# Layer 1's four spreads: from four products and copies to one product and four row broadcasts by DMA

## The chip, the core and the metric

The kernel runs on one core of one Trainium2 chip. The metric is device time in microseconds (us) of one execution. TensorE multiplies matrices (PE in the profile, its weight loads PEld), VectorE is DVE, ScalarE is ACT, GpSimd is POOL, and SyncE is SP, which here only issues DMAs.

## The reference, cut to what matters

Sixteen graphs of 512 nodes with 128 features pass through four graph layers, each behind a layer norm and a ReLU and added back to x. Layer 1 is the one that the change is about. Its attention has four heads of 32 features:

```python
h = (node_feats @ W.T + b).reshape(Bb, Nn, Hh, Cc)
l_src = jnp.einsum('bihc,hc->bih', h, a_src)
l_dst = jnp.einsum('bjhc,hc->bjh', h, a_dst)
logits = jax.nn.leaky_relu(l_src[:, :, None, :] + l_dst[:, None, :, :], ALPHA)
logits = jnp.where(adj_matrix[..., None] == 1, logits, NEG_INF)
probs = jax.nn.softmax(logits, axis=2)
out = jnp.einsum('bijh,bjhc->bihc', probs, h)
```

Layer 0 is the same with one head. Layer 2 mixes by sigmoids of products of node rows, layer 3 is three steps of a GRU over summed neighbours. `l_dst` of a head is one row of 512 numbers. The kernel wants that row in all 128 partitions, since partitions are the nodes i; this is the head's "spread".

## The kernel before, in words

One graph is handled in tiles of 128 partitions: four chunks c of 128 nodes, each a row of 512 neighbours. A graph goes through four stages: A (layer 0, bank `a_bank`), L (layer 1, banks `l0_bank` and `l1_bank`), B (layer 2) and C (layer 3). Each engine runs one list of (graph, step), sorted by a number from the tables `BEGIN` and `WHEN`. So the stages of neighbouring graphs interleave: while L of graph g runs, so do A of g+1, B and C of g-1. Nothing but semaphores ties one engine's place in its list to another's, and every engine takes its list strictly in order.

A unit is one head and one chunk, 16 in all for layer 1. For unit n, DVE does step `n` (`masked_max`, L611: spread minus mask, with the row maximum), then, once a head's four maxima are in, the shifts (L617 to L622) and step `v` (`logits`, L625). ACT exponentiates (L435), PE turns the result in an l bank (L879, step `q`), ACT copies it to `pT` (L443). Step `sum` (L968) uses all of it, and `x2` adds it to x.

Layer 1 begins with `stats1`, `norm1`, `rows1` (PE turns the normed rows into `l0_bank`, ACT copies them to `hT1`), then for each head h a step `dst`: PE multiplies `hT1` by `dst_rep[:, h, :]`, whose 128 columns are all the same, so all 128 partitions of the bank get the row (L934), and ACT copies it to one of two `spread` buffers (L427). `values1` (L686 to L693 on DVE) makes the values and the source terms. Heads 3 and 4 wait for a free buffer and a free bank in the middle of the units.

SP issues the loads of x, adj and the turned adj for all graphs, in program order: x of g+2, adj of g+1, turned adj of g. There is one buffer for adj (`adj_i`); `mask0`, `mask1`, `count` and `edges` read it.

## Time and profile before

| what | value |
|---|---|
| three runs | 1105.32, 1108.17, 1108.45 us, median 1108.17 |
| the profiled execution | 1104.81 us, its span 1103.0 us |
| PE busy | 959.7 us (87%) |
| DVE busy | 944.8 us (86%) |
| ACT busy | 885.0 us (80%) |
| POOL busy | 96.1 us (9%) |

The span is what the trace covers; the time holds 1.8 us more around it. The busy shares are means over the fill of the pipeline, thirteen even graphs in the middle, and the drain.

### The profile page before, as it was taken

The page shows a single profiled execution, that of the slowest core. Times are in us where ns is not written, and L with a number is a line of the kernel's source. Part 1 is how long each engine was busy: PE and PEld are TensorE (multiplying, and loading weights), DVE is VectorE, ACT ScalarE, POOL GpSimd, SP SyncE. Part 2 cuts the span into 40 slices and gives each one's busy share as a digit, 9 for nine tenths or more (in the row PEclk, how much of TensorE's full clock was granted, in tenths as well). Part 3 has the DMA queues.
Part 4 walks back from the last instruction along what each step waited for, and adds up shares of the span by engine and source line. Part 5 has one row for each costly group of instructions (what it writes and reads, how often), then busy time and mean ns, then how long its engine had stood idle before and what let it go on. Part 6 is the DMA issues. An engine that isn't in the chain of part 4 may idle for free.

```text
span 1103.0 us, 16049 instructions
## 1 busy us (share of the span) xinstructions
PE 959.7 (87%) x5024; PEld 613.6 (56%) x5024; DVE 944.8 (86%) x2710; ACT 885.0 (80%) x1876; POOL 96.1 (9%) x138
## 2 busy tenths in 40 slices
PE   4677898989989898998989898998989799898875
PEld 3453655656565565656566565656556465655443
DVE  5396989899898989999898989989898998988543
ACT  3477897979889797979889797988979798887643
POOL 0101010010001010100101011010101100000000
PEclk8678999999999999999999999999999999999989
DMA  2101111020111102011111102011110201101000
GB/s 89 50 37 48 39 48 48 11 86 11 39 49 48 49 11 87 10 41 47 48 49 48 50 10 79 18 40 49 48 49 10 87 1 40 48 1 48 1 10 10
DMA packets 34028, 43.92 MB, mean 40 GB/s; under 512 B 1040, under 2 KB 17424, under 8 KB 33936
## 3 DMA queue, kind: packets, MB, share of 16 engines
q1 hardware_dynamic: 25488, 38.61, 11.1%
q10 hardware_dynamic: 8448, 4.20, 1.3%
q8 instruction: 44, 0.72, 0.3%
q14 instruction: 48, 0.39, 0.1%
HBM read 38.61 MB, written 4.19 MB: 39 GB/s over the span
## 4 chain that ended last, share of the span: by engine, by line
PE 47%; DVE 36%; ACT 7%; issue 6%; POOL 3%; DMA 0%; DVEq 0%; ACTq 0%; SPq 0%; POOLq 0%
DVE probs L611 9%; PE l_bank L879 6%; DVE probs L625 6%; PE x_bank L968 5%; PE a_bank L911 4%; DVE sess L781 3%; PE r_bank L1029 3%; DVE sess L774 3%; PE n_bank L1029 2%; PE n_bank L1044 2%; ACT hn L367 2%; PE n_bank L1047 2%; PE l_bank L934 2%; PE r_bank L1032 2%; PE h_bank L1032 2%
## 5 line engine op out<-in xcount | busy, mean ns | idle before, releaser
L625 DVE SCALAR_TENSOR_TENSOR probs<-spread,s_lift,probs 128x512 f32<-128x512 f32 x320 | 232.9, 746 | 1.8
L611 DVE CUSTOM_DVE_ANT_0 probs<-spread,mask 128x512 f32<-128x512 f32 x320 | 211.9, 684 | 3.4 <-ACT spread L427 3.1
L443 ACT ACTIVATE pT<-l_bank 128x512 f32<-128x512 f32 x256 | 153.7, 600 | 40.9 <-PE l_bank L879 40.9
L435 ACT ACTIVATE probs<-probs,shift_p 128x512 f32<-128x512 f32 x256 | 185.0, 723 | 1.0 <-DVE probs L625 1.0
L879 PEld LDWEIGHTS l_bank<-ident,probs 128*128 128x128 f32 x1024 | 123.8, 144 | 78.8 <-issue 40.5
L879 PE MATMUL l_bank<-ident,probs 128*128 128x128 f32 x1024 | 155.0, 277 | 10.0 <-ACT probs L435 9.1
L349 POOL TENSOR_TENSOR rstd<-var_eps,power 128x4 f32<-128x4 f32 x64 | 72.8, 1137 | 961.0 <-DVE var_eps L605 636.3
L367 ACT ACTIVATE hn<-x,shift,rstd 128x128 f32<-128x128 f32 x192 | 79.4, 498 | 34.6 <-POOL shift L351 34.6
L934 PE MATMUL l_bank<-hT,dst_rep 128*128 128x512 f32 x128 | 72.1, 646 | 12.9 <-ACT pT L443 11.0
L427 ACT ACTIVATE spread<-l_bank 128x512 f32<-128x512 f32 x64 | 38.4, 600 | 42.2 <-PE l_bank L934 42.2
L1015 PE MATMUL y_bank<-hn,sess 128*128 128x128 f32 x512 | 64.3, 279 | 8.3 <-DVE sess L781 8.3
L1015 PEld LDWEIGHTS y_bank<-hn,sess 128*128 128x128 f32 x512 | 59.7, 192 | 15.1 <-DVE sess L781 15.1
L911 PE MATMUL a_bank<-values,pT 128*128 128x128 f32 x512 | 62.9, 283 | 0.7 <-ACT pT L400 0.7
L911 PEld LDWEIGHTS a_bank<-values,pT 128*128 128x128 f32 x512 | 61.3, 200 | 1.2 <-ACT pT L400 1.1
L968 PE MATMUL x_bank<-pT,values 128*32 128x512 f32 x512 | 61.2, 620 | 0.7 <-ACT pT L443 0.7
L804 DVE SCALAR_TENSOR_TENSOR hid_n<-r_t,hid_n 128x512 f32<-128x512 f32 x48 | 33.0, 687 | 28.0 <-ACT r_t L493 27.6
L435 ACT ACTIVATION_READ_ACCUMULATOR probs<-probs,shift_p 128x1 f32 x256 | 51.5, 201 | 0.0
L867 PE MATMUL x_bank<-ident,hn 128*128 128x128 f32 x128 | 21.4, 292 | 34.5 <-ACT hn L367 34.5
L1044 PE MATMUL n_bank<-edges,state_hi 128*128 128x512 f32 x128 | 44.6, 474 | 6.1 <-ACT state_hi L483 6.1
L879 PE MATMUL a_bank<-ident,probs 128*128 128x128 f32 x256 | 43.0, 294 | 7.8 <-ACT probs L395 4.6
L1032 PE MATMUL r_bank<-aggT,gi_w 128*128 128x512 f32 x96 | 49.3, 596 | 0.0
L1032 PE MATMUL h_bank<-aggT,gi_w 128*128 128x512 f32 x96 | 49.1, 593 | 0.0
(174 smaller groups left out, 2010.0 us busy)
## 6 DMA issues: line engine op xcount, KB each, us to landing
adj_i<-in_adj SPq DMA_DIRECT2D x16, 1024.0 KB, 5.1
adjt_i<-in_adj_t SPq DMA_DIRECT2D x16, 1024.0 KB, 5.5
xin<-in_x SPq DMA_DIRECT2D x16, 256.0 KB, 2.9
out<-out_sb ACTq DMA_DIRECT2D x16, 256.0 KB, 4.8
weights_sb<-in_weights SPq DMA_DIRECT2D x1, 840.0 KB, 4.6
```

What stands on the lines that cost most here:

```text
L349: g.tensor_tensor(rstd[n][:], var_eps[n][:], power[:], op=ALU.pow).then_inc(pool_step[n], 1)
L367: last = s.activation(hn[n][:, c, :], rows[:, c, :], ACT.Relu, bias=shift[n][:, c:c + 1], scale=rstd[n][:, c:c + 1])
L435: s.activation(row, row, ACT.Exp, bias=shift_p[:, head, c:c + 1], accum_out=den[:, head, c:c + 1]).then_inc(probs_ready, 1)
L443: s.activation(pT[:, head - 1, :, c * P:(c + 1) * P], l_banks[unit % 2][:, :].rearrange("p (j i) -> p j i", j=C), ACT.Copy).then_inc(pT_co ...
L611: chain.link(v.tensor_tensor_reduce(out=row, in0=spread_row, in1=mask, scale=1.0 / LIFT, scalar=-3e38, op0=ALU.subtract, op1=ALU.max, accu ...
L625: v.scalar_tensor_tensor(row, spread_row, source, row, ALU.min, ALU.subtract, reverse1=True).then_inc(ready, 1)
L879: last = t.transpose(dst[:, j * P:(j + 1) * P], row[:, j * P:(j + 1) * P], ident[:])
L911: last = t.matmul(a_bank[:, c * P:(c + 1) * P], pT0[:, j, c * P:(c + 1) * P], values0[:, j, :], start=(j == 0), stop=(j == C - 1))
L934: t.matmul(l_banks[head % 2][:, :], dst_rep[:, head, :], hT[1][:, :], start=True, stop=True).then_inc(dst_ready, 1)
L968: last = t.matmul(x_bank[h * HD:(h + 1) * HD, :], values1[:, j, h * HD:(h + 1) * HD], pT[:, h, j, :], start=(j == 0), stop=(j == C - 1), s ...
L1015: last = t.matmul(y_bank[:, c * P:(c + 1) * P], sess[:, j, c * P:(c + 1) * P], hn[2][:, j, :], start=False, stop=(j == C - 1), skip_group_ ...
L1032: t.matmul(bank[:, :], gi_w[:, layer, gate * D:(gate + 1) * D], aggT[:, :], start=start, stop=True).then_inc(gi_ready, 1)
```

## The change

- All four rows of `l_dst` come from one product: `dst_lift` holds four columns, one for each head, and the product fills four partitions of `a_bank`. ACT copies these 4x512 to `dst_rows` (step `dst1`).
- SP then issues four DMAs. Each reads one row of `dst_rows`, which lies in one partition, and writes it to all 128 partitions of `spread[:, h, :]`. There are four spread buffers now in place of two. A DMA of graph g also waits until the logits of that head of graph g-1 are done.
- `stats1`, `norm1`, `rows1` and `dst1` belong to stage A and use `a_bank`; the next graph's `rows0` waits for `dst_copied` where it waited for `x1_ready`. The turns of units no longer share the l banks with spread products.
- The tables `BEGIN` and `WHEN` are new for all engines.

```diff
+            def spread_rows(p):
+                sp.wait_ge(dst_copied, p.count(1, 1))
+                for h in range(H1):
+                    if p.before().exists():
+                        sp.wait_ge(logits_ready, p.before().count(UNITS, (h + 1) * C))
+                    sp.dma_start(spread[:, h, :],
+                                 dst_rows[h:h + 1, :].unsqueeze(1).to_broadcast([1, P, N])).then_inc(spread_loaded[h], 16)
+
...
                 if g + 2 < G:
                     load_x(Place(g + 2))
+                spread_rows(Place(g))
                 if g + 1 < G:
                     load_adj(Place(g + 1))
                 load_turned(Place(g))
...
+                elif step == "dst1":
+                    act.wait_ge(dst_ready, p.count(1, 1))
+                    if prev.exists():
+                        for h in range(H1):
+                            act.wait_ge(spread_loaded[h], prev.count(16, 16))
+                    s.activation(dst_rows[0:H1, :], a_bank[0:H1, :], ACT.Copy).then_inc(dst_copied, 1)
...
-                elif step[:3] == "dst":
-                    head = int(step[3])
-                    act.wait_ge(dst_ready, p.count(H1, head))
-                    if head > 2:
-                        act.wait_ge(logits_ready, p.count(UNITS, (head - 2) * C))
-                    elif prev.exists():
-                        act.wait_ge(logits_ready, prev.count(UNITS, (head + 2) * C))
-                    s.activation(spread[:, head % 2, :], l_banks[head % 2][:, :], ACT.Copy).then_inc(dst_copied, 1)
...
                     if c == 0:
-                        dve.wait_ge(dst_copied, p.count(H1, head))
+                        dve.wait_ge(spread_loaded[head - 1], p.count(16, 16))
...
+                elif step == "rows1":
+                    turn_rows(p, 1, a_bank)
+                elif step == "dst1":
+                    pe.wait_ge(hT_copied[1], p.count(1, 1))
+                    t.matmul(a_bank[0:H1, :], dst_lift[:, :], hT[1][:, :], start=True, stop=True).then_inc(dst_ready, 1)
```

SP's list at its start, before: x, the weights, adj and x of the first graphs, then for each graph the same three loads.

```order
L309 DMA xin<-in_x 128x4x128 [waits x1_ready]
L316 DMA adj_i<-in_adj 128x4x512 [waits edges_ready,count_ready,mask1_ready]
L321 DMA adjt_i<-in_adj_t 128x4x512
L309 DMA xin<-in_x 128x4x128 [waits x1_ready]
L316 DMA adj_i<-in_adj 128x4x512 [waits edges_ready,count_ready,mask1_ready]
L321 DMA adjt_i<-in_adj_t 128x4x512 [waits x3_ready]
```

The same place of SP's list now:

```order
L310 DMA xin<-in_x 128x4x128 [waits x1_ready]
L329 DMA spread<-dst_rows 128x1x512 [waits logits_ready,dst_copied]
L329 DMA spread<-dst_rows 128x1x512 [waits logits_ready] x3
L317 DMA adj_i<-in_adj 128x4x512 [waits edges_ready,count_ready,mask1_ready]
L322 DMA adjt_i<-in_adj_t 128x4x512 [waits x3_ready]
```

The four broadcasts of graph g stand ahead of the adj load of graph g+1 in one queue.

On ACT, the end of a graph's units before, from the copy of a late turn to the first spread of the next graph (`hn1` is norm1, `counted` is count, `avT` is step sum):

```order
L443 ACTIVATE pT<-l0_bank 128x4x128
L493 ACTIVATE r_t<-r_bank,gate_b 128x512
L443 ACTIVATE pT<-l1_bank 128x4x128
L367 ACTIVATE hn1<-x1,shift1,rstd1 128x128 x4
L497 ACTIVATE z_t<-n_bank,gate_b 128x512
L501 ACTIVATE n_t<-hid_n,gate_b 128x512
L413 ACTIVATE counted,count<-adj_i,minus_half 128x2048
L451 ACTIVATE avT<-x_bank 128x512
L373 ACTIVATE hT1<-l0_bank 128x512
L504 ACTIVATE state_hi<-h_bank 128x512
L427 ACTIVATE spread<-l1_bank 128x512
```

The same place now, from the exponential of the last unit (L445) to the copy of the four rows (L402):

```order
L445 ACTIVATE probs,den<-probs,shift_p 128x512
L377 ACTIVATE hn1<-x1,shift1,rstd1 128x128 x4
L453 ACTIVATE pT<-l0_bank 128x4x128
L453 ACTIVATE pT<-l1_bank 128x4x128
L503 ACTIVATE r_t<-r_bank,gate_b 128x512
L383 ACTIVATE hT1<-a_bank 128x512
L431 ACTIVATE counted,count<-adj_i,minus_half 128x2048
L507 ACTIVATE z_t<-n_bank,gate_b 128x512
L511 ACTIVATE n_t<-hid_n,gate_b 128x512
L461 ACTIVATE avT<-x_bank 128x512
L402 ACTIVATE dst_rows<-a_bank 4x512
```

norm1 stands earlier, and the rows' copy has taken the place of the first spread's copy.

On DVE, the last logits of a graph before (L625 x3), then the next graph's x1 and its statistics:

```order
L625 SCALAR_TENSOR_TENSOR probs<-spread,s1_lift,probs 128x512 x3
L660 TENSOR_SCALAR alive<-rmax 128x4
L661 RECIPROCAL rden<-den 128x4
L662 TENSOR_TENSOR rden<-rden,alive 128x4
L665 SCALAR_TENSOR_TENSOR x1<-a_bank,rden,xin 128x128 x4
L598 BN_STATS stats1<-x1 128x6 x4
L601 BN_AGGR moments1<-stats1 128x2 x4
L603 TENSOR_SCALAR minus_mean1<-moments1 128x4
L605 TENSOR_SCALAR var_eps1<-moments1 128x4
L598 BN_STATS stats0<-xin 128x6 x4
```

The same place now; the last L634 is the last unit's logits:

```order
L674 SCALAR_TENSOR_TENSOR x1<-a_bank,rden,xin 128x128 x4
L634 SCALAR_TENSOR_TENSOR probs<-spread,s1_lift,probs 128x512
L607 BN_STATS stats1<-x1 128x6 x4
L610 BN_AGGR moments1<-stats1 128x2 x4
L612 TENSOR_SCALAR minus_mean1<-moments1 128x4
L614 TENSOR_SCALAR var_eps1<-moments1 128x4
L634 SCALAR_TENSOR_TENSOR probs<-spread,s1_lift,probs 128x512
L607 BN_STATS stats0<-xin 128x6 x4
```

x1 and stats1 are done ahead of the last logits, where they came behind them. Between values1 and the first maximum of head 2 the order on DVE is what it was: four maxima, the four small instructions of the shifts, one logits. And `mask0`, the first reader of the next graph's adj on DVE, stood before `s0` to `s3`:

```order
L770 MEMSET cell2 128x1
L636 TENSOR_SCALAR mask0<-adj_i 128x2048
L774 SCALAR_TENSOR_TENSOR sess<-sess 128x512 x4
L781 SCALAR_TENSOR_TENSOR sess<-sess,adjt_i 128x512 x3
L812 SCALAR_TENSOR_TENSOR keep<-z_t,state 128x512
```

and stands behind `stats3` now:

```order
L836 SCALAR_TENSOR_TENSOR out_sb<-n_bank,x3 128x512
L796 SCALAR_TENSOR_TENSOR x3<-y_bank,x2 128x512
L607 BN_STATS stats3<-x3 128x6 x4
L610 BN_AGGR moments3<-stats3 128x2 x4
L612 TENSOR_SCALAR minus_mean3<-moments3 128x4
L616 TENSOR_SCALAR var_eps3<-moments3 128x4
L645 TENSOR_SCALAR mask0<-adj_i 128x2048
```

It is some 13 instructions of 128x512 later than before.

## Rows read from the trace of the kernel before

**Rows 1.** The page: busy time and share of each engine

```profile
PE 959.7 (87%) x5024; PEld 613.6 (56%) x5024; DVE 944.8 (86%) x2710; ACT 885.0 (80%) x1876; POOL 96.1 (9%) x138
```

**Rows 2.** Windows: stretch, its us, busy of each engine, PEclk, DMA share, GB/s

```profile
50.20:112.50 62.30, 48.53 (x238) 29.40 (x239) 51.75 (x160) 47.42 (x104) 4.68 (x6) 0.82 0.16 56
112.40:985.20 872.80, 796.50 (x4324) 513.70 (x4322) 801.07 (x2292) 752.85 (x1609) 81.42 (x110) 0.99 0.13 41
```

**Rows 3.** DVE's waits from 112.4 to 985.2: us in total, times, longest

```profile
DVE state_lo L820 <- ACT state_hi L504: 15.6, 14, 1.9
DVE keep L812 <- ACT z_t L497: 11.4, 12, 1.1
...
DVE probs L611 <- ACT spread L427: 2.4, 3, 0.8
```

**Rows 4.** The page's groups of spread products and spread copies

```profile
L934 PE MATMUL l_bank<-hT,dst_rep 128*128 128x512 f32 x128 | 72.1, 646 | 12.9 <-ACT pT L443 11.0
L427 ACT ACTIVATE spread<-l_bank 128x512 f32<-128x512 f32 x64 | 38.4, 600 | 42.2 <-PE l_bank L934 42.2
```

**Rows 5.** Timeline of DVE: start us, us, line, operation, out<-in

```profile
159.33 0.15 DVE L693 TENSOR_SCALAR other_kinds<-l_bank 128x1 int32<-128x1 f32 x1
...
583.88 2.07 DVE L625 SCALAR_TENSOR_TENSOR probs<-spread,s_lift,probs 128x512 f32<-128x512 f32 x3
585.87 0.16 DVE L660 TENSOR_SCALAR alive<-rmax 128x4 f32<-128x4 f32 x1
...
588.97 0.86 DVE L598 BATCH_NORM_STATS2 stats<-xin 128x6 f32<-128x128 f32 x4
...
590.43 0.68 DVE L804 SCALAR_TENSOR_TENSOR hid_n<-r_t,hid_n 128x512 f32<-128x512 f32 x1
...
602.11 0.15 DVE L693 TENSOR_SCALAR other_kinds<-l_bank 128x1 int32<-128x1 f32 x1
...
606.14 0.69 DVE L611 CUSTOM_DVE_ANT_0 probs<-spread,mask 128x512 f32<-128x512 f32 x1
...
985.22 0.15 DVE L693 TENSOR_SCALAR other_kinds<-l_bank 128x1 int32<-128x1 f32 x1
```

**Rows 6.** Timeline of ACT between two graphs' units

```profile
587.71 0.73 ACT L435 ACTIVATE probs<-probs,shift_p 128x512 f32<-128x512 f32 x1
...
588.41 0.70 ACT L489 ACTIVATE hid_n<-n_bank,half_bhn 128x512 f32<-128x512 f32 x1
...
589.46 0.71 ACT L493 ACTIVATE r_t<-r_bank,gate_b 128x512 f32<-128x512 f32 x1
590.03 0.63 ACT L443 ACTIVATE pT<-l_bank 128x512 f32<-128x512 f32 x1
590.50 1.67 ACT L367 ACTIVATE hn<-x,shift,rstd 128x128 f32<-128x128 f32 x4
592.04 0.71 ACT L497 ACTIVATE z_t<-n_bank,gate_b 128x512 f32<-128x512 f32 x1
592.61 0.75 ACT L501 ACTIVATE n_t<-hid_n,gate_b 128x512 f32<-128x512 f32 x1
593.23 2.03 ACT L413 ACTIVATE counted<-adj_i,minus_half 128x2048 bf16<-128x2048 int32 x1
...
595.68 0.60 ACT L373 ACTIVATE hT<-l_bank 128x512 f32<-128x512 f32 x1 [0.34 <-PE l_bank L867]
596.18 0.59 ACT L451 ACTIVATE avT<-x_bank 128x512 f32<-128x512 f32 x1
```

**Rows 7.** DMA view of 596 to 610 (40 slices), with one adj load

```profile
GB/s 0 0 0 0 0 0 0 0 0 0 0 0 0 0 0 0 0 0 0 0 70 146 111 246 374 410 410 380 439 310 123 0 0 0 0 0 0 0 0 0
...
q1 hardware_dynamic: 528, 1.05, 19.8%
...
adj_i<-in_adj SPq DMA_DIRECT2D x1, 1024.0 KB, 5.0
```

**Rows 8.** The page: a load of 256 KB, us from issue to landing

```profile
xin<-in_x SPq DMA_DIRECT2D x16, 256.0 KB, 2.9
```

More of the change, by code:

```diff
@@ L23 @@
 A_STEPS = (["stats0", "norm0", "rows0", "mask0", "dst0", "src0", "values0"] + [f"m{c}" for c in range(4)] + ["max0"]
-           + ["u0", "u1", "t0", "u2", "t1", "u3", "t2", "t3", "sum0", "x1"])
-L_STEPS = (["stats1", "norm1", "count", "rows1", "mask1", "dst1", "edges", "values1"]
-           + [f"n{c}" for c in range(4)] + ["max1", "dst2"]
+           + ["u0", "u1", "t0", "u2", "t1", "u3", "t2", "t3", "sum0", "x1",
+              "stats1", "norm1", "rows1", "dst1"])
+L_STEPS = (["count", "mask1", "edges", "values1"]
+           + [f"n{c}" for c in range(4)] + ["max1"]
            + [step for n in range(16)
-              for step in [f"v{n}"] + [f"q{n - 1}"] * (n > 0) + [f"dst{n // 4 + 3}"] * (n in (2, 6))
+              for step in [f"v{n}"] + [f"q{n - 1}"] * (n > 0)
               + [f"n{n + 4}"] * (n < 12) + [f"max{n // 4 + 2}"] * (n in (3, 7, 11))] + ["q15"])
@@ L217, in graph_layers @@
         probs0, probs = sb("probs0", [P, C, N]), sb("probs", [P, 2, C, N])
[L218 removed]
+        spread0, dst_rows = sb("spread0", [P, N]), sb("dst_rows", [P, N])
+        spread = sb("spread", [P, H1, N])
         pT0, pT = sb("pT0", [P, C, N]), sb("pT", [P, H1, C, N])
@@ L274, in graph_layers @@
         dst_ready, dst_copied = sem("dst_ready"), sem("dst_copied")
+        spread_loaded = [sem(f"spread_loaded{h}") for h in range(H1)]
         others_ready = sem("others_ready")
@@ L380, in step_a @@
                     copy_hT(p, 0, a_bank)
+                elif step == "norm1":
+                    norm(p, 1, x1[:, p.graph % 2, :, :])
+                elif step == "rows1":
+                    if prev.exists():
+                        act.wait_ge(val1_ready, prev.count(1, 1))
+                    copy_hT(p, 1, a_bank)
+                elif step == "dst1":
+                    act.wait_ge(dst_ready, p.count(1, 1))
+                    if prev.exists():
+                        for h in range(H1):
+                            act.wait_ge(spread_loaded[h], prev.count(16, 16))
+                    s.activation(dst_rows[0:H1, :], a_bank[0:H1, :], ACT.Copy).then_inc(dst_copied, 1)
                 elif step == "dst0":
@@ L404, in step_l @@
                 prev = p.before()
-                if step == "norm1":
-                    norm(p, 1, x1[:, p.graph % 2, :, :])
-                elif step == "rows1":
-                    copy_hT(p, 1, l_bank0)
-                elif step == "count":
+                if step == "count":
                     act.wait_ge(adj_loaded, p.count(16, 16))
@@ L572, in constants @@
                 cw.own(v.tensor_copy(head_parts[:, :, :].rearrange("p a h -> p (a h)"), l_bank1[:, 16:16 + 2 * H1]))
-                for h in range(HEADS):
-                    last = v.tensor_scalar(dst_rep[:, h, :], ones[:], dst_w[:, h:h + 1], LIFT, ALU.mult, ALU.mult)
-                cw.own(last)
+                v.tensor_scalar(dst_lift[:], dst_w[:, 1:HEADS], LIFT, None, ALU.mult)
+                cw.own(v.tensor_scalar(dst_rep[:, :], ones[:], dst_w[:, 0:1], LIFT, ALU.mult, ALU.mult))
             def more_constants():
@@ L667, in step_a @@
                     last.then_inc(x1_ready, 1)
+                elif step == "stats1":
+                    dve.wait_ge(x1_ready, p.count(1, 1))
+                    sums(p, 1, x1[:, par, :, :], ca)
             def step_l(p, step):
@@ L671, in step_l @@
                 prev = p.before()
-                if step == "stats1":
-                    dve.wait_ge(x1_ready, p.count(1, 1))
-                    sums(p, 1, x1[:, par, :, :], cl)
-                elif step == "mask1":
+                if step == "mask1":
                     dve.wait_ge(adj_loaded, p.count(16, 16))
@@ L717, in step_l @@
                         dve.wait_ge(shift_ready, p.count(H1, head))
-                    logits(probs[:, head % 2, c, :], spread[:, head % 2, :], s1_lift[:, head, c:c + 1], logits_ready)
+                    logits(probs[:, head % 2, c, :], spread[:, head - 1, :], s1_lift[:, head, c:c + 1], logits_ready)
             def kinds_of(p, k):
```

53 lines of the change are left out of this document (18 added, 35 removed), and 96 rows, old and new, of the table WHEN.

## The prediction

> **What bounds the kernel now.** I read the page's busy line first [rows 1]: PE 87%, DVE 86%, ACT 80%, so no engine is full over the span. The windows correct that [rows 2]: from 112.4 to 985.2 us, DVE is busy 801.07 of 872.8 us and PE 796.50. Then I looked for DVE's waits in that stretch [rows 3]: the largest are for `state_hi` (15.6 us) and `z_t` (11.4 us). All rows of that answer, of which three stand there, add up to 52 us. So DVE has something to do nearly always. Its own small gaps behind dependent instructions make up the rest. The period of the pipeline is the distance of one instruction that each graph has once, `other_kinds`: (985.22 - 159.33) / 13 = 63.5 us [rows 5]. DVE's list is what sets it. The spreads themselves cost DVE 2.4 us of waits in thirteen graphs [rows 3]. The long idle time before their copies on ACT (42.2 us) and the 72.1 us of products on PE [rows 4] lie beside DVE's work.
>
> **What the change takes away.** Four products and four copies become one each. On PE that is three quarters of 72.1 us, 54 us; on ACT three quarters of 38.4 us, 29 us [rows 4]. DVE loses nothing: same maxima, same logits. What PE and ACT give up can only come back as less waiting of DVE, at most the 52 us. I value it at 10 us, since the two largest waits are chains in layer 3 that the change does not shorten.
>
> **What it adds: when head 2 has landed.** The new path is dst_rows on ACT, then a DMA for each head. I count from the end of the last logits of a graph (585.87 in the trace [rows 5]).
>
> ACT must do, in the order shown for the change, the steps from the last exponential to the rows' copy. Start to start [rows 6]: the exponential 0.70, norm1 1.54, two copies 0.47 each, `r_t` 0.57, `hT1` 0.50, count 2.1, `z_t` 0.57, `n_t` 0.62, `avT` 0.5, and 0.6 for the copy itself [rows 4]: 8.6 us. With some 0.4 us of hand-over, `dst_rows` is there 9.0 us after the last logits.
>
> DVE, in the same stretch, has less to do than before. Before, head 2's first maximum started at 606.14, 20.3 us after 585.87. x1 and stats1 (585.87 to 588.97, 3.1 us [rows 5]) now stand ahead of the last logits. So DVE could start head 2 at 17.2 us.
>
> Now the copy of one row into 128 partitions. The trace before has no such DMA: its loads touch 128 partitions with every packet's two ends spread out. So I bound it. A load of the same 256 KB lands in 2.9 us [rows 8]; the adj load, four times as large, in 5.0 us [rows 7]. That is the lower end: if reading one partition 128 times is as good as reading memory, all four heads are there 5 us after the issue. The upper end: all 512 packets of a graph read four neighbouring partitions, and may be served one after the other. The adj load used 19.8% of 16 engines over 14 us for 528 packets, 84 ns for a packet of 2 KB [rows 7]; 128 of them in a row take 10.8 us. By rate rather than packet time: at its best the adj load moved 439 GB/s, 27.4 GB/s for each of 16 engines [rows 7]. If one partition gives what one engine takes, a head takes D = 262144 B / 27.4 GB/s = 9.6 us. I take 9.6, since in every load of the trace the sixteen engines work on sixteen different pieces of SBUF, and here all of them want the same one; a rate for one place is nearer to one engine's rate than to sixteen's.
>
> The Trainium skill, SBUF — State Buffer, "Door 1: The DMA port swizzle", says that DMA rate depends on how many of 16 ports the partitions reach, and gives 27.6 GB/s measured for partitions 0..3, which are one port. By it a head would take 9.5 us and the forecast would stay. The same skill, DMA: Bandwidth & Descriptors, "Anatomy of one DMA", prices a DMA at 2.0 us plus bytes over 436 GB/s; by that a head would land in 2.6 us, and the first rival below would be the forecast. No row of this trace decides between the two; that is what the experiment must do.
>
> A landing has a fixed part: the adj load's 5.0 us less its packets' 0.198 x 14 = 2.8 us, so 2.2 us [rows 7]. Head 2 lands at 9.0 + 2.2 + 2 x 9.6 = 30.4 us. DVE wanted it at 17.2. **It waits 13.2 us** in total, split over the first maxima of heads 1 and 2 (head 1 lands at 20.8, and its four maxima, the shifts and one logits stand between). Everything behind it on DVE waits too, that is the whole list. Heads 3 and 4 land at 40.0 and 49.6. Between the first maximum of head 2 and that of head 3 lie about 21 instructions of 0.66 us (the three logits in [rows 5] take 1.99), 14 us, so head 3 is wanted at 44 us and is no wait.
>
> **The adj load behind it.** It stands in the same queue behind the four broadcasts. Its packets can start when theirs are through: it lands at 9.0 + 2.2 + 4 x 9.6 + 2.8 = 52.4 us. `mask0` wants it 26 instructions of 0.66 us and one stats (588.97 to 590.43, 1.46 us [rows 5]) behind head 2's first maximum, at 30.4 + 18.6 = 49.0. **Another 3.4 us.** Were there no late broadcasts this load would be hidden, as it is before.
>
> **The sum.** 13 full periods x 16.6 = 216 us. The two periods ahead of 159.33 and the last graph's units take the 13.2 only: 40 us. Less the 10 us from above: +246 us. On the profiled execution (1104.8 us, span 1103.0 and 1.8 around it) that is 1351; on the median of the three runs, 3.4 us higher, **1354 us**. With D = 10.8 the two waits are 15.6 and 5.8, the sum 278 + 47 - 10, the time 1423. With D = 8.5 they are 11.0 and 1.2, the time 1290.
>
> **Rivals.**
> 1. *The broadcasts are as fast as a load.* All land 5 us after issue, at 14 us, before DVE wants even head 1 (17.2 less 4.0 for four maxima, shifts and one logits: 13.2). It decides at 9.0 + 2.2 + 2D = 17.2, D = 3.0 us. Below it there is no wait, and PE's and ACT's 83 us less work can shorten DVE's waits. A third to a half of the 52 us would be 17 to 26 us, so 1090 us; if none comes back it is 1108. For it: the row of the same size, 2.9 us [rows 8]. Against: that row reads memory and not one partition.
> 2. *Partly shared:* one partition serves more than one engine's worth, D between 3 and 8.5. With D = 6, head 2 lands at 23.2, a wait of 6.0 in all 16 graphs, and adj in time: 1108 + 96 - 10 = 1194 us. For it: nothing in the trace says that an engine's rate is a partition's limit.
> 3. *Slower than one engine's rate*, say twice D: the four heads take 77 us, more than the period; head 2 lands at 49.6, 32 us late, and the time is beyond 1600.
> 4. *The clock.* Where PE was busy 48.53 of 62.3 us, the granted clock was 0.82, and 0.99 where it was busy 796.5 of 872.8 [rows 2]. With a period of 80 us and less work, PE would be busy 70%. If it then falls to 1.2 GHz in part, the chain to dst_rows, which has the product of step sum in it, grows by up to 3 us a graph, 50 us in all. I leave it in the range.
>
> **Chances.** One at a time, D between 8.5 and 11.5: 0.52, its own range 1290 to 1430. Partly shared 0.18. As fast as a load 0.18. Slower still 0.12. The range to hold the time 8 times in 10 must reach into the fast case: 1090 to 1430. Faster by over 0.3% (about what a measurement of this kernel can tell from no change): 0.15, from the fast case; within 0.3%: 0.04; slower: 0.81.
>
> **What would show it.** In the profile after: DMA `spread<-dst_rows`, 256 KB, with a median landing of about 12 us for a single one and far more for the fourth behind the others (right), or 3 us (rival 1). DVE's longest waits would be the maxima L620 for a DMA, 13 us a graph, then `mask0` L645 for the adj load, 3 us. `other_kinds` 80 us apart. DVE's busy time unchanged near 945, PE's near 906, ACT's near 856. The prediction is wrong if the wait is there but elsewhere in the list absorbs it, or if D is not what one engine takes; then every us of D moves the time by 32 us up to D = 8, and by 64 above.

## The result, and the profile after

| | median | runs | profiled span | granted clock |
|---|---|---|---|---|
| before | 1108.31 us | 4 (1105.32 to 1110.95) | 1103.0 us | 0.97 |
| after | 1384.87 us | 4 (1379.25 to 1386.62) | 1383.1 us | 0.84 |

The changed kernel takes 1.249 times as long (interval 1.244 to 1.2535), 277 us more. The prediction was 1354 us, with a range of 1090 to 1430.

The page of the kernel after: the busy line, the ends of the chain that ended last, one group of instructions, and two of the DMA issues with the median time to their landing.

```profile
PE 999.4 (72%) x4912; PEld 661.9 (48%) x4928; DVE 942.8 (68%) x2707; ACT 875.1 (63%) x1828; POOL 101.9 (7%) x138
DMA 31%; DVE 19%; ACT 16%; PE 14%; SPq 11%; issue 6%; POOL 2%; DVEq 0%; ACTq 0%; POOLq 0%
...
L620 DVE CUSTOM_DVE_ANT_0 probs<-spread,mask 128x512 f32<-128x512 f32 x320 | 212.4, 686 | 99.7 <-DMA spread<-dst_rows 98.3
...
adj_i<-in_adj SPq DMA_DIRECT2D x16, 1024.0 KB, 26.0
spread<-dst_rows SPq DMA_DIRECT2D x64, 256.0 KB, 22.3
```

Against [rows 1], DVE does the same work (942.8 us for 944.8) in a longer span, so its share falls from 86% to 68%. PE is busy for more us than before, not for fewer, although its list is shorter: the granted clock is 0.84 where it was 0.97, and the mean matmul is longer (301 ns for a turn of the units, 277 before). The chain no longer runs over engines alone. Transfers hold 31% of it and SP's issues 11%.

DVE's waits over the whole span of the kernel after (total us, times, longest):

```profile
DVE cell L779 <- DVEq L776: 99.5, 16, 8.2
DVE probs L620 <- DMA spread<-dst_rows: 98.3, 20, 7.1
DVE mask L645 <- DMA adj_i<-in_adj: 69.0, 15, 10.0
DVE hid_n L813 <- ACT r_t L503: 55.7, 20, 6.6
DVE n_t L824 <- ACT n_t L511: 21.5, 15, 1.6
```

The second and third rows are the two waits that the prediction named. The first is not: `cell` L779 is a memset that stands behind DVE's load of `other_kinds` into a register (the load tells DVE whether it must do a rare part). That load is one that the kernel before has too. The view of the tile `other_kinds` in the kernel after (duration in ns min/median/max, first and last start in us):

```profile
L702 DVE TENSOR_SCALAR other_kinds<-l_bank x16: 146/150/155, 51.0 to 1251.7; 128x1 int32<-128x1 f32 x16
L759 DVEq TENSOR_LOAD <-other_kinds x16: 306/6820/7836, 128.3 to 1328.2; - x16
L990 PEldq TENSOR_LOAD <-other_kinds x16: 304/6768/7821, 138.1 to 1331.5; - x16
```

A register load that took 308 ns on DVE before (the same view, median) takes 6820 ns now. The first row gives the mean distance of graphs, (1251.7 - 51.0) / 15 = 80.0 us. The prediction's 63.5 + 16.6 = 80.1 was for the last thirteen distances only; by the starts in the timeline these are (1251.75 - 204.67) / 13 = 80.5 us, and they are uneven, 72 to 91 us, where before's are 63 to 65.

One graph in the timeline of the kernel after, first DVE and ACT, then SP's queue (start us, us, ..., idle time before and what ended it):

```profile
674.12 0.75 DVE L634 SCALAR_TENSOR_TENSOR probs<-spread,s_lift,probs 128x512 f32<-128x512 f32 x1
...
683.72 0.59 ACT L402 ACTIVATE dst_rows<-a_bank 4x512 f32<-4x512 f32 x1 [0.21 <-PE a_bank L900]
...
688.86 0.15 DVE L702 TENSOR_SCALAR other_kinds<-l_bank 128x1 int32<-128x1 f32 x1
696.11 0.69 DVE L620 CUSTOM_DVE_ANT_0 probs<-spread,mask 128x512 f32<-128x512 f32 x1 [7.10 <-DMA spread<-dst_rows]
...
704.65 0.06 DVE L779 MEMSET cell<- 128x1 f32 x1 [6.01 <-DVEq L776]
...
706.09 0.68 DVE L620 CUSTOM_DVE_ANT_0 probs<-spread,mask 128x512 f32<-128x512 f32 x1
...
729.05 1.23 DVE L645 TENSOR_SCALAR mask<-adj_i 128x2048 bf16<-128x2048 int32 x1 [4.08 <-DMA adj_i<-in_adj]
```

```profile
684.33 17.56 SPq L329 DMA_DIRECT2D spread<-dst_rows  x4
702.00 9.49 SPq L317 DMA_DIRECT2D adj_i<-in_adj  x1
```

The last logits end at 674.79, `dst_rows` is ready at 684.31, and head 1's spread is used at 696.11, 11.8 us behind its issue. DVE stood idle from 689.01 to 696.11 for it. Then four maxima, then 6.0 us for the register load. Head 2's maximum (706.09) comes 0.7 us after the shifts, without a wait of its own.

The DMA view of the same graph, 684 to 735 us (40 slices: busy tenths of the 16 DMA engines, then GB/s; then the broadcasts' KB and median us to landing):

```profile
DMA  0988999888899999899889998888997999991000
GB/s 0 37 26 26 29 27 29 26 26 26 26 27 29 29 27 29 26 27 27 26 26 32 27 27 26 26 26 26 27 34 39 318 389 364 394 327 50 12 0 0
...
spread<-dst_rows SPq DMA_DIRECT2D x4, 256.0 KB, 25.4
```

This is what happens to the transfers, in two lines: some 37 us at 26 to 29 GB/s while the four broadcasts go, then over 300 GB/s for the adj load that had stood behind them. The sixteen engines are busy for 80% or more of nearly every slice in both stretches, so it is not that few of them take part in a broadcast.

### The profile page after: what moved, and what is told of

Its sections match the earlier page's. It is cut to its first block, busy times and chain, and to the rows that moved or that the text cites. A ratio compares the mean times of both kernels' runs of the same rounds, so it can differ in the third digit from the quotient of the medians.

```text
span 1383.1 us, 15808 instructions
## 1 busy us (share of the span) xinstructions
PE 999.4 (72%) x4912; PEld 661.9 (48%) x4928; DVE 942.8 (68%) x2707; ACT 875.1 (63%) x1828; POOL 101.9 (7%) x138
## 4 chain that ended last, share of the span: by engine, by line
DMA 31%; DVE 19%; ACT 16%; PE 14%; SPq 11%; issue 6%; POOL 2%; DVEq 0%; ACTq 0%; POOLq 0%
DMA adj_i<-in_adj 28%; SPq L329 11%; DVE probs L620 4%; DVE probs L634 3%; PE a_bank L925 3%; ACT hn L377 2%; DMA spread<-dst_rows 2%; ACT probs L417 2%; POOL rstd L359 2%; ACT counted L431 2%; PE l_bank L888 2%; DVE stats L607 2%; ACT pT L453 2%; ACT pT L422 1%; PE n_bank L1041 1%
## 5 line engine op out<-in xcount | busy, mean ns | idle before, releaser
L620 DVE CUSTOM_DVE_ANT_0 probs<-spread,mask 128x512 f32<-128x512 f32 x320 | 212.4, 686 | 99.7 <-DMA spread<-dst_rows 98.3
L445 ACT ACTIVATE probs<-probs,shift_p 128x512 f32<-128x512 f32 x256 | 185.2, 724 | 110.3 <-DVE probs L634 110.1
L634 DVE SCALAR_TENSOR_TENSOR probs<-spread,s_lift,probs 128x512 f32<-128x512 f32 x320 | 234.6, 748 | 2.2
L888 PE MATMUL l_bank<-ident,probs 128*128 128x128 f32 x1024 | 175.1, 301 | 56.7 <-ACT probs L445 54.6
L888 PEld LDWEIGHTS l_bank<-ident,probs 128*128 128x128 f32 x1024 | 135.7, 156 | 123.9 <-ACT probs L445 83.6
L359 POOL TENSOR_TENSOR rstd<-var_eps,power 128x4 f32<-128x4 f32 x64 | 87.4, 1366 | 1234.6 <-DVE var_eps L614 693.0
L1012 PE MATMUL y_bank<-hn,sess 128*128 128x128 f32 x512 | 92.6, 358 | 81.5 <-DVE sess L790 81.2
L477 ACT ACTIVATE sess<-sess 128x512 f32<-128x512 f32 x64 | 38.9, 627 | 124.9 <-DVE sess L783 124.9
L1012 PEld LDWEIGHTS y_bank<-hn,sess 128*128 128x128 f32 x512 | 88.4, 269 | 44.2 <-DVE sess L790 44.1
L906 PE MATMUL a_bank<-hT,dst_rep 128*128 128x512 f32 x32 | 32.6, 1122 | 81.8 <-issue 81.0
L881 PE MATMUL a_bank<-weights_sb,hT 128*128 128x128 f32 x128 | 32.3, 432 | 80.0 <-DVE s_lift L648 80.0
L779 DVE MEMSET cell<- 128x1 f32 x16 | 0.9, 59 | 99.5 <-DVEq L776 99.5
L881 PEld LDWEIGHTS a_bank<-weights_sb,hT 128*128 128x128 f32 x128 | 27.7, 320 | 84.0 <-DVE s_lift L648 84.0
L645 DVE TENSOR_SCALAR mask<-adj_i 128x2048 bf16<-128x2048 int32 x16 | 19.6, 1227 | 69.0 <-DMA adj_i<-in_adj 69.0
L445 ACT ACTIVATION_READ_ACCUMULATOR probs<-probs,shift_p 128x1 f32 x256 | 51.2, 200 | 0.0
```

Of the source, the lines that this page charges most:

```text
L359: g.tensor_tensor(rstd[n][:], var_eps[n][:], power[:], op=ALU.pow).then_inc(pool_step[n], 1)
L445: s.activation(row, row, ACT.Exp, bias=shift_p[:, head, c:c + 1], accum_out=den[:, head, c:c + 1]).then_inc(probs_ready, 1)
L620: chain.link(v.tensor_tensor_reduce(out=row, in0=spread_row, in1=mask, scale=1.0 / LIFT, scalar=-3e38, op0=ALU.subtract, op1=ALU.max, accu ...
L634: v.scalar_tensor_tensor(row, spread_row, source, row, ALU.min, ALU.subtract, reverse1=True).then_inc(ready, 1)
L881: last = t.matmul(dst[:, c * width:(c + 1) * width], hT[n][:, c * P:(c + 1) * P], of, start=True, stop=True)
L888: last = t.transpose(dst[:, j * P:(j + 1) * P], row[:, j * P:(j + 1) * P], ident[:])
```

## The experiments

A theory and rivals. **T**: sixteen DMA engines that all read one partition (or its neighbours) get no more than about one engine's rate; all else follows from the lateness of the transfers. **R1**: what costs is the register load, which the transfers slow, and not the wait for the spread. **R2**: the new orders and banks cost by themselves. **R3**: a DMA's fixed cost, or the number of DMAs or packets, does it. Where nothing is said the compared kernel is before, run on the same chip (medians 1110.98 to 1113.33).

### The same rows in 128 partitions

`dst_lift` has 128 columns, so that `dst_rows` holds head p mod 4 in partition p; each head is four DMAs that read 32 partitions each. Orders and banks are those of after. (The product costs PE hardly more for it: the mean of its matmuls is 648 ns with 4 columns in after, 707 with 128 in this run and 637 with 128 in the last run below.)

```diff
-                    sp.dma_start(spread[:, h, :],
-                                 dst_rows[h:h + 1, :].unsqueeze(1).to_broadcast([1, P, N])).then_inc(spread_loaded[h], 16)
+                    for k in range(H1):
+                        sp.dma_start(spread[k:P:H1, h, :], dst_rows[h:P:H1, :]).then_inc(spread_loaded[h], 16)
...
-                    t.matmul(a_bank[0:H1, :], dst_lift[:, :], hT[1][:, :], start=True, stop=True).then_inc(dst_ready, 1)
+                    t.matmul(a_bank[:, :], dst_lift[:, :], hT[1][:, :], start=True, stop=True).then_inc(dst_ready, 1)
```

> The changed kernel, but the one product has 128 columns (column p for head p mod 4), so that each row of dst_rows lies in 32 partitions, and each head is copied by four DMAs of 32 partitions each, from 32 different partitions. It computes all that the changed kernel computes. Bytes, destinations and orders are the same. If the cost is that all 16 engines read one partition's port (27 GB/s), a head lands about 3 us after its issue, the waits of DVE for spreads (98 us), for the adj load (69 us) and behind the register load (99 us) all go, and the time is 1085 to 1110 us. If what is slow is copying from SBUF to SBUF as such, or DVE's new order, it stays above 1300 us.

Measured: 1129.25 us (6 runs), ratio 1.0167 (1.0134 to 1.02). DVE's waits of this run:

```profile
DVE hid_n L814 <- ACT r_t L503: 57.1, 20, 7.3
DVE n_t L825 <- ACT n_t L511: 20.7, 15, 1.6
```

There is no wait for a spread and none for adj, and the register load takes 310 ns (median). So the same bytes to the same places, read from many partitions, take away 257 us of the loss (the difference of the ratios, 1.2488 - 1.0167 = 0.232, of before's 1108). T holds; the register load falls with it. What remains is 0.0167 of 1108, 18.5 us (16 us by the medians of this chip), and it points to R2: with the new orders DVE waits 57.1 us for `r_t` where it waited 27.6 before, and 20.7 for `n_t` (before 2.9). Against these 47 us more stand 10 us less behind `state_hi` L830 (10.4 for 20.4) and 8 less behind `z_t` (6.9 for 15.2). No run separates the orders from the banks, from SP's sixteen issues or from the granted clock, which is 0.93 here and 0.96 to 0.97 in before. The time missed what was expected (1085 to 1110): I had again taken the freed PE and ACT for a gain.

### The register load from another partition

```diff
-                    others = dve.value_load(other_kinds[0:1, par:par + 1])
+                    others = dve.value_load(other_kinds[64:65, par:par + 1])
```

and the same on PE.

> The changed kernel, with the register loads of other_kinds (DVE and PE, median 6.8 us after, 0.3 us before) reading partition 64 in place of partition 0; the value is the same in all partitions. If they are slow because partition 0 hangs on the port that the broadcasts drain, they take 0.3 us again and the 99.5 us of DVE behind them go. What DVE gains there it should then wait for head 2, which lands at about the same moment, so by my theory the time stays within 1.5% of 1385 us. By the rival, in which the register load is a cost of its own, it falls by up to 99 us, to about 1290 us.

Measured: 1387.62 us, ratio 1.2485 (1.2427 to 1.2544). The loads still take 5544 ns on DVE and 5352 on PE. DVE's waits:

```profile
DVE probs L620 <- DMA spread<-dst_rows: 114.8, 32, 7.0
DVE cell L779 <- DVEq L776: 80.2, 16, 7.0
```

19.3 us less behind the register load and 16.5 us more for the spreads. So the time stays, as expected, but the loads do not go back to 0.3 us. Distance from partition 0 helps little, and what it helps is given back at the next wait.

### No register load at all

The load and the branch on it are taken out on both engines, and with them the rare part of layer 2 for other kinds.

```diff
-                    others = dve.value_load(other_kinds[0:1, par:par + 1])
-                    with dve.If(others != 0):
+                    if False:
```

> The changed kernel without its register loads and the branch on them: the part for adjacencies with other kinds of edges, which these inputs do not have, is left out. e2 showed that the loads are slow from partition 64 too (5.5 us), so it did not take their wait away. Here it is gone. If head 2 lands at about the moment at which the load comes back, DVE waits for the spread in its place and the time stays within 1% of 1385 us. If the load is a cost of its own, it falls by up to 99 us.

Measured: 1380.83 us, ratio 1.2424 (1.2368 to 1.2479). DVE's waits:

```profile
DVE probs L620 <- DMA spread<-dst_rows: 179.8, 31, 7.1
```

R1 falls in this kernel. The 99.5 us behind the register load are gone, and the wait for spreads has grown from 98.3 to 179.8, with 13.5 us more before two of these maxima that the profile ascribes to no releaser. Head 2's maximum now waits for what the memset had covered. By the ratios the load's own price is 7 us, and the two intervals overlap.

### Half of each row, and a sixteenth

The broadcasts copy 256 columns in one run and 32 in the other; the other columns of `spread` stay at zero, so the softmax is of other numbers. Four DMAs for a graph as in after.

```diff
-                    sp.dma_start(spread[:, h, :],
-                                 dst_rows[h:h + 1, :].unsqueeze(1).to_broadcast([1, P, N])).then_inc(spread_loaded[h], 16)
+                    sp.dma_start(spread[:, h, 0:256],
+                                 dst_rows[h:h + 1, 0:256].unsqueeze(1).to_broadcast([1, P, 256])).then_inc(spread_loaded[h], 16)
```

> The changed kernel, with each broadcast copying 256 of the 512 columns (the others stay zero from a memset at the start, so half of each spread is left out). If the cost goes by bytes through one port, a head takes 4.8 us in place of 9.6, head 2 lands at 9.5 + 2.2 + 9.6 = 21.3 us after the last logits, 4.1 us after DVE wants it, and the adj load is in time: 1108 + 16 x 4.1 = 1174 us, between 1150 and 1200. If it goes by packets, whose number is unchanged, the time stays at 1385 us.

> The changed kernel, with each broadcast copying 32 of the 512 columns (15/16 of each spread is left out and stays zero). All waits, semaphores, products, copies and orders stay. By bytes a head takes 0.6 us, by the other account unchanged 9.6 us. It gives what the rest of the change is worth without its transfers: my prediction values what PE and ACT give back at 10 us, so 1090 to 1108 us; if the new orders were themselves the trouble it would be above 1120 us.

Measured: 1231.83 us, ratio 1.1071 (1.1025 to 1.1117), and 1149.49 us, ratio 1.0329 (1.0294 to 1.0363). The shortest landing is 6.9 us with half the bytes and 2.7 with a sixteenth, where it is 11.7 with all: 2.2 us and 9.5 us for each 256 KB give 7.0, 2.8 and 11.7. The numbers of DMAs and of packets are those of after. So it goes by bytes, and R3 falls. Waits of DVE with half the bytes:

```profile
DVE cell L782 <- DVEq L779: 85.6, 16, 7.5
...
DVE probs L623 <- DMA spread<-dst_rows: 13.3, 8, 2.2
```

and with a sixteenth:

```profile
DVE cell L782 <- DVEq L779: 25.0, 13, 3.3
```

Both times are higher than I expected (1150 to 1200, and 1090 to 1108), and these rows say why: where head 2 is hardly late (13.3 us in all), the register load is a price of its own, 85.6 us. Even with a sixteenth of the bytes this kernel lies 20 us above the one that reads many partitions (1149.49 and 1129.25), beside 25.0 us of that wait where the other has 7.5. Nothing covers it there. These two runs were not repeated without the register load, so this rests on the rows alone.

### The adj load in another queue

ACT issues the next graph's adj load behind `edges`, so that it does not stand behind the broadcasts in SP's queue.

```diff
-                if g + 1 < G:
-                    load_adj(Place(g + 1))
...
+                    if p.graph + 1 < G:
+                        act.wait_ge(mask1_ready, p.count(1, 1))
+                        act.wait_ge(count_ready, p.count(1, 1))
+                        act.wait_ge(edges_ready, p.count(1, 1))
+                        s.dma_start(adj_i[:], rows(adj, p.graph + 1)).then_inc(adj_loaded, 16)
```

> The changed kernel, with the adj load of the next graph issued by ACT behind the step edges, on ACT's queue, so that it no longer stands behind the four broadcasts in SP's queue. If mask0's wait (69 us, 4.6 a graph) comes from standing behind them, it goes, and the time falls by 50 to 69 us, to about 1325 us. If the engines are simply full, each of its packets takes turns with a broadcast's packet of 1.08 us, 33 of them for an engine is 36 us, and mask0 waits as long as before or longer.

Measured: 1330.37 us, ratio 1.1965 (1.1913 to 1.2018). By the ratios (1.2488 - 1.1965) that is 58 us less than after, and about what was expected. mask0's wait falls from 69.0 us to 3.7. The load itself still takes 23.6 us to land (median; 5.1 before), which I put down to its sharing the engines with the broadcasts, but it starts early enough. The second wait of the prediction was real, and came from the queue.

### Broadcasts by themselves

Two small programs without any graph work, only DMAs of 256 KB and a few register loads (so their times, 306.01 and 188.68 us, one execution each, say nothing about the kernel). In the first, SP copies one row to 128 partitions, alone or together with ACT, whose row lies in the same partition or in 1, 4 or 64.

```diff
+                both(n)
+                sp.dma_start(left[:, :], spread(0)).then_inc(left_done, 16)
...
+                nc.scalar.dma_start(right[:, :], spread(4)).then_inc(right_done, 16)
```

> No graph is computed; the kernel only copies one row of 2 KB into 128 partitions, alone and in pairs, from SP's and ACT's queues at once, each pair three times: source partitions 0 and 0, 0 and 1, 0 and 4, 0 and 64; then 128 partitions into 128, and 64 into 64; and DVE loads a register while a broadcast runs. Alone a broadcast lands in 11.7 us. If one partition is the limit, 0 and 0 land in about 21 us and all other pairs in 12. If a group of partitions shares the limit, 0 and 1 take 21 us too, and 0 and 64, in different groups, 12. If each of the 16 engines is the limit (it waits for its own slow reads), all four pairs take 21 us. 128 into 128 should land in about 3 us. The register load should take 0.3 us with nothing running and 5 to 7 us beside a broadcast, for partition 64 as for partition 0.

Alone a broadcast lands in 11.1 us, 128 partitions to 128 in 2.3. Of a pair the first lands in 11.1 to 11.8 us and the second in 20.7 (partition 0), 20.7 (1), 18.5 (4) and 18.8 (64). Two rows far apart, each a DMA of its own, hardly go side by side. Of the three accounts above, none fits as it stands: 0 and 1 agree with a group that shares a limit, but 4 and 64 should then have landed in 12 us, and their 18.5 and 18.8 lie nearer to the third account's 21, in which the engines wait for their own slow reads. No register load shows in this program's trace.

The second program reads several rows in one DMA and writes to memory, one DMA after another.

```diff
+                sp.dma_start(away(4, 1), spread(src[0:4, :])).then_inc(left_done, 16)
...
+                sp.dma_start(away(4, 2), spread(src[0:16:4, :])).then_inc(left_done, 16)
...
+                sp.dma_start(away(16, 3), spread(src[0:16, :])).then_inc(left_done, 16)
...
+                sp.dma_start(away(16, 4), spread(src[0:128:8, :])).then_inc(left_done, 16)
```

> No graph is computed. One DMA of 256 KB at a time, three times each: partition 0 into 128 partitions of SBUF (11.1 to 11.8 us in e10); then into memory from partition 0 alone; from partitions 0 to 3; from 0, 4, 8, 12; from 0 to 15; from 0, 8, ..., 120. If one partition is the limit (27 GB/s), the second goes four times as fast for either set of four, about 4.5 us, and 16 partitions take 2.5 to 3 us in both forms. If neighbouring partitions share the limit, 0 to 3 take 11 us as one does, 0, 4, 8, 12 take 4.5, and 0 to 15 take 4.5. DVE also loads a register and branches on it: 0.3 us with nothing running, and 5 to 7 us beside the broadcast, for partition 64 as for partition 0, if what it shares with the DMAs is not partition 0's own port (e2); otherwise only for partition 0.

SP's queue in this run; each issue waits for the DMA before it, so the distance of two starts is the time of the first. L62 reads partition 0 alone, L65 partitions 0 to 3, L68 0, 4, 8 and 12, L71 0 to 15, L74 every eighth of 128:

```profile
25.80 0.58 SPq L62 DMA_DIRECT2D out<-src  x1
37.02 0.80 SPq L65 DMA_DIRECT2D out<-src  x1
49.04 0.67 SPq L68 DMA_DIRECT2D out<-src  x1
53.33 0.62 SPq L71 DMA_DIRECT2D out<-src  x1
57.59 0.57 SPq L74 DMA_DIRECT2D out<-src  x1
60.57 11.66 SPq L59 DMA_DIRECT2D left<-src  x2
```

So 11.2, 12.0, 4.3, 4.3 and 3.0 us for the same 256 KB. Four neighbouring partitions are as slow as one; four partitions four apart are as fast as sixteen neighbours. These DMAs do not all keep the same number of engines busy. Here are stretches from the middle of the first four (us, DVE, POOL, PEclk, busy share of the 16 DMA engines, GB/s):

```profile
29.00:36.00 7.00, 0.00 (x0) 0.00 (x0) 1.00 0.86 27
40.00:47.00 7.00, 0.00 (x0) 0.00 (x0) 1.00 0.23 26
51.20:52.80 1.60, 0.00 (x0) 0.00 (x0) 1.00 0.26 102
55.20:57.00 1.80, 0.00 (x0) 0.00 (x0) 1.00 0.89 101
```

L65 and L68, the clean pair, both have about four engines' worth of work (0.23 and 0.26 of sixteen) and differ by four in rate, so the source's partitions make the difference. Between L62 and L65 the busy share falls to a quarter and the rate stays, and so it does between L71 and L68: more engines do not help. The limit belongs to a group of partitions on the reading side, and it is the same for partition 0 whether SBUF or memory is written (11.1 and 11.2 us). The Trainium skill, SBUF — State Buffer, "Door 1: The DMA port swizzle", assigns partitions 0 to 3 to one port, 0 to 15 to four, and every eighth to eight; the five times agree with that. The pairs of the first program don't follow from this mapping alone: 4 and 64 are on other ports than 0 there, and yet the second landed at 18.5 and 18.8 us.

DVE's register loads in the same program (ns min/median/max), L106 from partition 0 and L113 from partition 64 beside a broadcast, L95 and L98 the same two with no DMA about:

```profile
L106 DVEq TENSOR_LOAD <-index x3: 7585/7593/7676, 6.3 to 120.6; - x3
L113 DVEq TENSOR_LOAD <-index x3: 6284/6523/6550, 17.6 to 132.0; - x3
...
L95 DVEq TENSOR_LOAD <-index x1: 542/542/542, 1.6 to 1.6; - x1
L98 DVEq TENSOR_LOAD <-index x1: 527/527/527, 2.4 to 2.4; - x1
```

### ACT's order, with the rows in 128 partitions

The first experiment left 57.1 and 20.7 us of waits for `r_t` and `n_t`. Here `count` is moved behind `n_t` on ACT, and in a second run norm1 behind `r_t` as well.

```diff
+        for g in range(2, graphs):
+            for what, behind in [("count", "g1_mix")]:
+                steps.remove((g, what))
+                steps.insert(steps.index((g - 2, behind)) + 1, (g, what))
```

> e1_many_rows (1129 us, 1.017 of before, its transfers no longer waited for), with one step of ACT's list moved for graphs 2 to 15: count (2.2 us) goes behind n_t of the same place, as it stood before the change, where e1 has it ahead of z_t and n_t. In e1 DVE waits 20.7 us for n_t (before: 2.9) and 6.9 for z_t. If the rest of the loss is ACT's new order at this place, that wait goes and the time falls by about 1 us a graph, to 1113 us, the time of before. If it is a matter of DVE's order or of bank a, the wait only moves and the time stays within 0.3% of 1129.

> As e6_count_behind, and norm1 (1.6 us) also goes behind r_t, ahead of which it stands in e1. In e1 DVE waits 57.1 us for r_t (before: 27.6), 26.1 of it in the 13 even periods. If ACT's order is the cause, both waits go and the time is 1095 to 1110 us, under before, by the work that the single product saves. The rival: norm1 is then late for rows1 and the product, dst_rows are copied later, and the time is the same as that of e6 or above it.

Measured: 1135.81 us, ratio 1.0215 (1.018 to 1.025), and 1165.48 us, ratio 1.0482 (1.0445 to 1.052). Neither fell, as I had hoped (1113, and 1095 to 1110). The second is clearly slower than without the move, the first by so little (1.0167, up to 1.02) that the intervals touch. The wait for `n_t` did go, from 20.7 us to 3.1, but DVE waits elsewhere; from the first of these runs:

```profile
DVE x L756 <- PE y_bank L980: 34.3, 15, 9.7
```

Without the move that wait was 10.1 us. In the second run it is 39.9, and the one for `z_t` is 38.6 where it was 6.9. A wait that was taken away by a swap came out again elsewhere. Which part of the new orders costs the time stays open.

### The old orders

The first experiment's rows and broadcasts, with before's tables and before's banks: norm1, rows1 and the product are back in L.

> The kernel before, with its own orders and with norm1, rows1 and the product of layer 1 in the l banks as they were, but with one product for all four heads and the broadcasts from 32 partitions as in e1_many_rows; the steps dst2 to dst4 are gone. e1 is 1.7% above before with hardly a wait for a DMA. If that loss is the new orders and the move to bank a, this one has none of it, and PE and ACT have 83 us less work than before: 1095 to 1113 us, no slower than before. If it is the path through the DMA itself (dst_rows are there at 598.4 in the trace of before, head 1's four copies land some 4 us later, at the 602.2 where DVE wants it), it stays at about 1129 us.

Measured: 1188.42 us (7 runs), ratio 1.0694 (1.0658 to 1.073), far above what I expected. DVE's waits and SP's queue around one graph:

```profile
DVE mask L646 <- DMA adj_i<-in_adj: 52.8, 15, 5.2
...
DVE probs L621 <- DMA spread<-dst_rows: 9.9, 13, 2.2
```

```profile
579.63 10.13 SPq L331 DMA_DIRECT2D spread<-dst_rows  x16
589.87 0.52 SPq L318 DMA_DIRECT2D adj_i<-in_adj  x1
```

Sixteen issues take SP 10.1 us. The adj load is issued only behind them, and the old orders want `mask0` early. So the last run, otherwise the same, issues one DMA for each head, which reads its 32 partitions four times:

```diff
-                    for k in range(H1):
-                        sp.dma_start(spread[k:P:H1, h, :], dst_rows[h:P:H1, :]).then_inc(spread_loaded[h], 16)
+                    sp.dma_start(spread[:, h, :],
+                                 dst_rows[h:P:H1, :].unsqueeze(1).to_broadcast([P // H1, H1, N])).then_inc(spread_loaded[h], 16)
```

> The orders and banks of before, one product with 128 equal-by-four columns, so that dst_rows holds each head's row in 32 partitions, and now one DMA for each head in place of four: it reads each of the 32 partitions four times. SP issues 4 broadcasts for a graph in place of 16. My theory for the run with the old orders and 16 broadcasts (1188 us) is that SP's 10 us of issues push the adj load too late for mask0: then SP's issues take under 4 us here, mask0's 52.8 us of waits for the adj load fall under 10 us, a broadcast lands in 3 to 5 us, the register load stays at 0.3 us, and the time is 1115 to 1145 us; the waits for the spreads and in layer 3 (hid_n, state_hi) stay. Rival A: with the old orders the adj load is too late behind the rows' copy in any case: mask0 still waits 40 us or more and the time is 1175 to 1195 us. Rival B: reading one partition four times slows its packets as reading it 128 times did: landings of 6 us and more, a register load above 1 us, and a time above 1150 us with the wait at the first maxima. If it comes out below before's own time, the idea of the change pays once the reads are spread out.

Measured: 1106.91 us (12 runs, 1105.28 to 1109.82) beside 1110.98 (17 runs), ratio 0.9964 (0.9947 to 0.9982), better than I expected (1115 to 1145) and the only kernel here below before. The margin is thin: the fastest runs of both are 1105.28 us. Its waits (none for a spread or for adj), its queue and the DMA view of 600 to 612 us:

```profile
DVE hid_n L814 <- ACT r_t L503: 32.0, 11, 7.0
DVE state_lo L830 <- ACT state_hi L514: 20.6, 18, 2.0
DVE keep L822 <- ACT z_t L507: 15.5, 16, 1.2
```

```profile
601.65 2.49 SPq L330 DMA_DIRECT2D spread<-dst_rows  x4
605.36 0.37 SPq L318 DMA_DIRECT2D adj_i<-in_adj  x1
```

```profile
GB/s 0 0 0 0 0 0 0 0 0 184 396 362 389 376 382 382 389 375 260 0 0 89 280 48 239 375 369 389 396 403 403 369 123 14 0 0 0 0 0 0
...
spread<-dst_rows SPq DMA_DIRECT2D x4, 256.0 KB, 2.5
```

Four DMAs with the bytes and destinations of those that took 37 us at 27 GB/s take 3 us at 380, since their source is 32 partitions and not one. SP is done with the issues after 2.49 us. That removed 81 us by the medians. The two traces lie 73.1 us apart (spans 1178.8 and 1105.7; the first is of the fastest of its seven runs), and the waits account for them: 62.7 for adj and the spreads, and 12.0 less behind `r_t` (36.3 to 32.0), L797 (5.5 to 1.3) and `out_sb` (4.2 to 0.7). The gain over before is small because DVE's waits are those of before (`state_hi` 20.6 for 20.4 us, `z_t` 15.5 for 15.2), and its work is the same. PE's 17 us and ACT's 21 us less work are hardly seen in the time. PE has even lost 54 us of spread products (72.1 to 17.7), but its other matmuls take 37 us more: the granted clock of the profiled run is 0.94 where it was 0.97 before, and a turn of the units takes 288 ns for 277. What that lower clock costs in time was not tried.

## Why the prediction was right

The time alone says little for the prediction, since the range of 1090 to 1430 us also held its first two rivals. What bears it out is the landing of one broadcast and the two waits.

**The bound and the period.** DVE's list sets the time, a wait of DVE is paid in full: right. The period of the last thirteen distances came out at 80.5 us for 80.1. The agreement is partly luck: with broadcasts from many partitions the same distances are 64.8 us and not 63.5, so the late transfers made 15.7 us of the period, where I had 16.6, and the rest came from a term that I had with the other sign.

**When dst_rows is ready.** 9.0 us after the last logits predicted, 9.5 in the graph shown (684.31 - 674.79). Right, and in that graph the lower clock cost this chain half a us at most.

**The copy of one row.** D = 9.6 us and 2.2 us fixed predicted, 11.8: the smallest landing is 11.7 us, the bare broadcast 11.1. Right, and the choice of one engine's rate over the row of a 256 KB load [rows 8] carried the forecast. The reason that I gave, one place in SBUF for all sixteen engines, is shown by the first and the last experiment. The place is a group of neighbouring partitions, by the small program, and the number of engines does not matter there. The Trainium skill, SBUF — State Buffer, "Door 1: The DMA port swizzle", has 27.6 GB/s for partitions 0 to 3; the trace's 26 to 29 GB/s agree. The price of the Trainium skill, DMA: Bandwidth & Descriptors, "Anatomy of one DMA", 2.0 us plus bytes over 436 GB/s, which that section fits to DMAs of the gpsimd path (these are SP's), gives an estimate of 2.6 us. The last experiment's 2.5 us agree with it, and the 11.7 us of this source do not.

**The wait for heads 1 and 2.** 13.2 us for a graph, split over the two heads. The size is nearly right: over the run it is (98.3 + 99.5) / 16 = 12.4 us, of which before had 0.5 (its 5.1 and 3.1 us). Head 1's part by the prediction's own numbers is 20.8 - 13.2 = 7.6 us, and it is 7.1 in the graph shown. The other 5.6 us were to be head 2's wait. They fell to the register load instead (6.0 us), which the prediction did not have. It cost hardly more, since head 2 would have waited then anyway; that is what the run without the load shows.

**The adj load.** 3.4 us predicted, 69.0 / 15 = 4.6 measured; moving the load to another queue gave 58 us back, where the forecast has 13 x 3.4 = 44. Right in its cause, a quarter short in its size.

**What the change takes away.** This term failed: -10 us predicted, and nothing for the new orders and banks. The first experiment, in which DVE waits for no spread and no adj load, is 18.5 us slower than before by its ratio. The last experiment, with the old orders, is 4 us faster (0.36% of 1108), and that is about what the freed PE and ACT gave. The new orders put `r_t` and `n_t` later for DVE, and together with the banks they cost more than that relief. So the term is about +18, and the transfers are worth 257 us where the sum had 216 + 40 = 256. The forecast's 31 us of error are nearly all this one term. That 257 meets 256 so closely is luck as well: the spreads' wait was forecast too long (16 x 13.2 = 211 us for some 190), and adj's too short (44 for 69).

**The rivals.** The fast one and the partly shared one are refuted by the landing, and so is one slower than an engine's rate. The clock did fall, to 0.84, but the chain that it was to lengthen, the one to dst_rows, is only 0.5 us longer than forecast. Its own price was not measured. It does spoil one of the signs: PE's busy time was to be near 906 us and is 999.4, and ACT's is 875.1 for 856. DVE's 942.8 for 945 is as forecast. And the price of D above 8 us was given as 64 us for each us of D, where the sum itself has 16 x 2 + 13 x 2 = 58.

## What to carry to other kernels

A DMA that reads one partition, or four neighbours, ran at one engine's rate here (27 GB/s) and held up everything queued behind it; price it by that rate, and price what stands behind it too. If a row must go to all partitions by DMA, have the product write it to many partitions first and let one DMA read them all; then it was as fast as a load (2.5 us for 256 KB, x's load 2.8). And work taken off engines that do not set the time is worth little until a run shows otherwise (4 us here for 54 and 29 us of work), while new orders have a price of their own.

## What the runs showed that I had not expected

- A register load on DVE or PE takes 0.3 us in the kernel before and 6.8 beside the broadcasts (7.6 in the small program), also from partition 64 (5.5 and 6.5). With half the bytes it was 6.6 us, with a sixteenth 2.1 on DVE. With broadcasts from many partitions it is back at 0.3. Why a load waits at all, and why one from another partition does too, stays open.
- SP's own issues are held up: of the four broadcasts' issues in the graph shown the first two take 0.5 and 0.6 us, the third 6.75 and the fourth 9.6, the time of one broadcast. The adj load's issue takes 9.5 us where it takes 0.4 in the last experiment.
- A quick issue has a price as well: about 0.63 us each, 10.1 us for sixteen.
- Two broadcasts in two queues from partitions 0 and 4 (or 64) hardly overlap, while one DMA that reads 0, 4, 8 and 12 takes 4.3 us and not 11.2. The pair of 0 and 4 keeps 0.87 to 0.89 of the sixteen engines busy at 27 to 35 GB/s, the one DMA only 0.26 at 102. The first of the pair lands as soon as it does alone, so most of the second's bytes seem to come behind it. What separates the two cases was not tried.
